# Weight preparation without GpSimd, scale copies in DRAM, and single modulations in a two-layer feed-forward kernel

## The reference

```python
# x (64, 64, 512), cond (64, 256); b2, b3, b_up, b_down are biases
q_emb = relu(cond @ W3 + b3)                                   # one gate per batch and feature
z     = (64 * x + sum_n(x)) * q_emb[:, None, :]
x1    = relu(z @ W2 + b2)
w_up   = ((w_up_q - 7.5)   * repeat(w_up_scale, 64, axis=1)).T      # 512 x 2048
w_down = ((w_down_q - 7.5) * repeat(w_down_scale, 64, axis=1)).T    # 2048 x 512
x2  = relu(x1 @ w_up + b_up + x1 @ up_a @ up_b)
out = x + x2 @ w_down + b_down + x2 @ down_a @ down_b
```

## Time and profile before

| | |
|---|---|
| median of three runs | 848.18 us (842.65 to 849.38) |
| the profiled execution's own time | 847.49 us |
| its span, first to last instruction | 845.7 us, mean granted TensorE clock 0.968 |
| busy: TensorE, VectorE, ScalarE, GpSimd | 767.0, 553.7, 422.1, 95.5 us |

### The profile page before, as it was taken

The page is one execution under the profiler, slowest core; times in us unless marked ns, Lnnn a source line. Parts: engine busy times, 40 slices in busy tenths (PEclk is TensorE's granted clock), DMA queues, the critical chain, the costliest instruction groups (busy, mean ns, idle before and its releaser), DMA issues.

```text
span 845.7 us, 9583 instructions
## 1 busy us (share of the span) xinstructions
PE 767.0 (91%) x3248; PEld 620.2 (73%) x3248; DVE 553.7 (65%) x705; ACT 422.1 (50%) x734; POOL 95.5 (11%) x81
## 2 busy tenths in 40 slices
PE   6379887878889999999999999998999999999997
PEld 5268665766668787777778887787878886888875
DVE  5665547646556567766677679575866769666575
ACT  3856234535534526375665726565755544343441
POOL 2441132232221202000000002000000002000000
PEclk9789999999899999999999999999999999999999
DMA  9714675775765659666551678565650786665552
GB/s 304 275 47 138 210 232 155 232 215 173 212 175 164 211 187 396 202 208 224 175 174 50 235 242 319 200 203 197 208 188 27 258 304 239 210 184 177 199 172 100
DMA packets 92144, 169.55 MB, mean 200 GB/s; under 512 B 8768, under 2 KB 25280, under 8 KB 91456
## 3 DMA queue, kind: packets, MB, share of 16 engines
q1 hardware_dynamic: 91808, 168.86, 60.8%
q10 hardware_dynamic: 288, 0.08, 0.0%
HBM read 129.05 MB, written 39.85 MB: 200 GB/s over the span
## 4 chain that ended last, share of the span: by engine, by line
PE 58%; DVE 14%; DMA 12%; ACT 8%; issue 5%; SPq 3%; DVEq 0%; ACTq 0%
PE ps L1073 19%; PE ps L1074 19%; PE ps L1075 19%; DMA scale<-in_scales 12%; ACT xt L364 4%; DVE x_lo L891 3%; DVE made L758 2%; DVE whole L749 2%; SPq L264 1%; DVE x_sum L795 1%; DVE x2p_lo L766 1%; ACT xm_hi L376 1%; SPq L258 1%; DVE xt L720 1%; DVE res L781 1%
## 5 line engine op out<-in xcount | busy, mean ns | idle before, releaser
L1073 PE MATMUL ps<-x_hi,ring 128*128 128x512 f32 x672 | 266.4, 396 | 18.6 <-ACT ps L481 10.2
L1074 PE MATMUL ps<-x_lo,ring 128*128 128x512 f32 x672 | 264.2, 393 | 0.0
L1075 PE MATMUL ps<-x_hi,ring 128*128 128x512 f32 x672 | 264.0, 393 | 0.0
L1073 PEld LDWEIGHTS ps<-x_hi,ring 128*128 128x128 f32 x672 | 127.6, 190 | 54.2 <-ACT ps L481 14.2
L1075 PEld LDWEIGHTS ps<-x_hi,ring 128*128 128x128 f32 x672 | 127.7, 190 | 26.9
L1074 PEld LDWEIGHTS ps<-x_lo,ring 128*128 128x128 f32 x672 | 127.7, 190 | 25.9
L364 ACT ACTIVATE xt<-xt,gated,gate_n 128x64 f32<-128x64 f32 x224 | 76.7, 428 | 104.5 <-DVE gated L714 104.5
L891 DVE TENSOR_TENSOR x_lo<-x_sum,x_hi 128x512 fp32r<-128x512 f32 (+1 forms) x96 | 82.8, 883 | 12.6 <-ACT x_hi L497 8.6
L473 ACT ACTIVATE f<-ps,bias 128x512 f32<-128x512 f32 x96 | 64.7, 690 | 41.2 <-PE ps L1075 41.2
L851 DVE TENSOR_TENSOR res<-ps,res 128x512 f32<-128x512 f32 x72 | 48.5, 688 | 30.7 <-PE ps L1075 30.7
L822 DVE TENSOR_TENSOR ps<-s,ps 128x512 f32<-128x512 f32 x48 | 33.3, 693 | 52.4 <-PE ps L1075 48.0
(11 more groups left out here) (79 smaller groups left out, 1049.9 us busy)
## 6 DMA issues: line engine op xcount, KB each, us to landing
ring<-made_w SPq DMA_DIRECT2D x336, 256.0 KB, 3.8
made_w<-made SPq DMA_DIRECT2D x16, 1280.0 KB, 5.9
xt<-in_x SPq DMA_DIRECT2D x32, 256.0 KB, 5.4
code<-in_codes SPq DMA_DIRECT2D x16, 512.0 KB, 7.6
scale<-in_scales SPq DMA_DIRECT2D x32, 256.0 KB, 8.2
res<-in_x SPq DMA_DIRECT2D x4, 2048.0 KB, 9.8
made_w<-plain SPq DMA_DIRECT2D x64, 128.0 KB, 6.1
out<-res SPq DMA_DIRECT2D x12, 512.0 KB, 5.7
```

The costliest lines, as they stand in the source:

```text
L1073: pe.matmul(dest, w_hi, a_hi, start=start, stop=False, skip_group_check=True)
L1074: pe.matmul(dest, w_hi, a_lo, start=False, stop=False, skip_group_check=True)
L1075: return pe.matmul(dest, w_lo, a_hi, start=False, stop=stop, skip_group_check=True)
```

## The change

1. Scales: one DMA early in the prologue copies each scale row eight times into a DRAM tensor `made_s`; each unit's scales are then one DMA that reads 16 rows, each eight times. A third scale buffer lies in the space of `s4`.
2. SyncE's loop of stage 1: `load_scale(u+4)` and `load_codes(u+3)` stand ahead of the two stores of unit u; `load_res(0)` moves into the loop.
3. GpSimd has no instruction left. Its sums (`made_totals`), the low parts of W2 and of the tables, and the residual fix (`fix_c22`, four operations of 512 columns a block, two by each of the first D slots) are VectorE's. The tables lie in three quadrants instead of four with a smaller part to split, and the wide one is cast and split in two pieces.
4. The prologue's order is written out anew: gates in four PSUM banks with a signal each; of the second half, eighth 5 is modulated on VectorE; `low_rank(0)` stands behind the first step of the second half, `low_rank(1)` behind the last, and `low_rank(u+2)` behind the second tile of unit u instead of ahead of unit u.
5. Stage 1's loops on VectorE and ScalarE are reordered (below); block 1's input is modulated in units 4 to 11.
6. Blocks 1 and 2: one modulation in each of the slots 3, 4, 6, 7, 8, 10, 11, 12; sum and gate stand right behind `share`; the input loads begin at slot 0 instead of 3.
7. Last block: ("U", 7) stands ahead of ("D", 2, 0); the operands of units 6 and 7 get buffers of their own in the space of x1, free after the last product of ("U", 7), and their steps are reordered.

```diff
-            ("U", 5), ("U", 6), ("D", 2, 0), ("U", 7), ("D", 2, 1), ("D", 3, 0), ("D", 3, 1)]
+            ("U", 5), ("U", 6), ("U", 7), ("D", 2, 0), ("D", 2, 1), ("D", 3, 0), ("D", 3, 1)]
...
+    MODULATED = [3, 4, 6, 7, 8, 10, 11, 12]
+
+
+    def x2_set(s, p):
+        return p % 2 + (2 if s == SBS - 1 and p >= NP - 2 else 0)
...
+        x2_place = [("x2", 0), ("x2", 28672), ("x1", 0), ("x1", 28672)]
+        x2_hi = [sb(f"x2_hi{v}", [P, 7, T], F32R, over, skip) for v, (over, skip) in enumerate(x2_place)]
...
+        made_s = nc.dram_tensor("made_s", [UNITS, 2, COPIES, 1024], F32, kind="Internal").ap()
...
             def load_scale(u):
-                if u >= 2:
-                    sp.wait_ge(dequantized, u - 2 + 1)
-                for h in range(2):
-                    sp.dma_start(scale[u % 2][64 * h:64 * h + 64, :],
-                                 scales[uid(FIRST[u]), h:h + 1, :].to_broadcast([64, 1024])).then_inc(scale_loaded[u % 2], 16)
+                if u >= 3:
+                    sp.wait_ge(dequantized, u - 3 + 1)
+                rows = made_s[uid(FIRST[u])].rearrange("h c v -> (h c) v").unsqueeze(1)
+                sp.dma_start(scale[u % 3][:], rows.to_broadcast([2 * COPIES, P // 2 // COPIES, 1024])).then_inc(scale_loaded[u % 3], 16)
...
+                if k == 1:
+                    sp.dma_start(made_s, scales.unsqueeze(2).to_broadcast([UNITS, 2, COPIES, 1024])).then_inc(scales_copied, 16)
...
+            load_x(0, KD)
+            load_x(0, KD + 1)
             load_codes(0)
+            sp.wait_ge(scales_copied, 16)
             load_scale(0)
-            for k in range(KD):
-                load_x(0, KD + k)
-            load_codes(1)
-            load_scale(1)
-            load_codes(2)
+            load_x(0, KD + 2)
+            load_x(0, KD + 3)
+            for u in (1, 2):
+                load_codes(u)
+                load_scale(u)
             sp.wait_ge(w2_split, KD)
             for k in range(KD):
                 sp.dma_start(made_w2[k], w2_in_ring[k][:].rearrange("p h v -> p (h v)").bitcast(F32)).then_inc(w2_stored, 16)
-            sp.wait_ge(tab_split, 3)
-            load_res(0)
+            load_scale(3)
             for u in range(UNITS):
-                if u + 2 < UNITS:
-                    load_scale(u + 2)
+                if u + 4 < UNITS:
+                    load_scale(u + 4)
+                if u + 3 < UNITS:
+                    load_codes(u + 3)
+                if u == 0:
+                    sp.wait_ge(tab_split, 3)
+                    load_res(0)
                 store_plain(u)
                 if 2 <= u < 10:
                     load_x(1, u - 2)
                 store_made(u)
-                if u + 3 < UNITS:
-                    load_codes(u + 3)
...
-                    if s < SBS - 1 and 3 <= n < 11:
-                        load_x(s + 1, n - 3)
+                    if s < SBS - 1 and n < 8:
+                        load_x(s + 1, n)
...
-                if p >= 2:
+                if x2_set(s, p) >= 2:
+                    act.wait_ge(prod[M6], chain_no(s, ("U", NP - 1)) + 1)
+                elif p >= 2:
...
                     if unit[0] == "U":
                         full_tile(u, 0)
+                        full_tile(u, 1)
+                    if 4 <= u < 12:
+                        x_modulate(1, u - 4)
+                    if u >= 12:
+                        x_high(1, 2 * (u - 12))
+                        x_high(1, 2 * (u - 12) + 1)
                     made_high(u)
-                    if unit[0] == "U":
-                        full_tile(u, 1)
-                    if 3 <= u < 11:
-                        x_modulate(1, u - 3)
-                    if 11 <= u < 13:
-                        x_high(1, 2 * (u - 11))
-                        x_high(1, 2 * (u - 11) + 1)
                     if unit[0] == "U":
                         full_tile(u, 2)
...
+            def made_totals(u):
+                w = whole[u % 3][:].rearrange("p (i q a c) -> p i q a c", i=2, q=2, a=2)
+                to = made_sum[:, u % 2, :, 1, :].rearrange("p v (q c) -> p v q c", q=2)
+                dve.wait_ge(whole_done, 2 * u + 2)
+                if u >= 2:
+                    dve.wait_ge(made_stored[u % 2], 16 * (u // 2))
+                dve.tensor_tensor(to[:, 0:2].rearrange("p a q c -> p q a c"), w[:, 0], w[:, 1], ALU.add).then_inc(made_summed, 1)
+                dve.tensor_tensor(to[:, 2], w[:, 0, :, 0, :], w[:, 1, :, 1, :], ALU.add).then_inc(made_summed, 1)
+                dve.tensor_tensor(to[:, 3], w[:, 0, :, 1, :], w[:, 0, :, 0, :], ALU.subtract).then_inc(made_summed, 1)
+                dve.tensor_tensor(to[:, 4], w[:, 1, :, 0, :], w[:, 1, :, 1, :], ALU.subtract).then_inc(made_summed, 1)
...
+            def fix_c22(s, dd):
+
+                to = res[:, dd + 2, 1, :]
+                dve.wait_ge(res_loaded, 16 * s + 16)
+                dve.tensor_tensor(to, to, res[:, dd, 1, :], ALU.subtract).then_inc(res_fixed, 1)
+                dve.wait_ge(res_fixed, 4 * (s - 1) + 2 * dd + 1)
+                dve.tensor_tensor(to, to, res[:, dd + 2, 0, :], ALU.add).then_inc(res_fixed, 1)
...
+            x_low(0, 3)
+            lora_low()
+            wide_low(slice(0, T), 2)
+            x_sum(0, 5)
+            x_shift(5)
+            x_modulate(5)
+            x_sum(0, 6)
+            x_gate(0, 6)
+            x_sum(0, 7)
+            x_gate(0, 7)
+            dequantize(0)
+            x_low(0, 4)
+            add_lora(0)
+            x_low(0, 5)
+            x1p_low(0, 0)
+            x1p_low(0, 2)
+            x_low(0, 6)
+            dequantize(1)
+            x_low(0, 7)
+            plain_low(0)
...
+            wide_low(slice(T, NH * P), 3)
+            add_lora(1)
             x1p_low(1, 0)
             x1p_low(1, 2)
-            add_lora(1)
+            made_totals(0)
...
                 if u < 14:
                     plain_low(u + 1)
-                    if u + 2 < UNITS:
-                        dequantize(u + 2)
                 evacuate(u, 0)
-                if u + 2 < UNITS:
-                    add_lora(u + 2)
                 evacuate(u, 1)
+                if 4 <= u < 12:
+                    x_sum(1, u - 4)
+                    x_gate(1, u - 4)
+                if u < 14:
+                    dequantize(u + 2)
+                if 12 <= u < 14:
+                    x_low(1, 2 * (u - 12))
+                    x_low(1, 2 * (u - 12) + 1)
                 if u < 14:
                     made_low(u)
+                    add_lora(u + 2)
                 if u == 14:
                     x1_lows_late(1)
-                if 3 <= u < 11:
-                    x_sum(1, u - 3)
-                    x_gate(1, u - 3)
                 evacuate(u, 2)
-                if 11 <= u < 13:
-                    x_low(1, 2 * (u - 11))
-                    x_low(1, 2 * (u - 11) + 1)
                 evacuate(u, 3)
+                if u < 14:
+                    made_totals(u + 1)
...
+                    if not last and n in MODULATED:
+                        x_sum(s + 1, MODULATED.index(n))
+                        x_gate(s + 1, MODULATED.index(n))
+                    if unit[0] == "D" and unit[1] == 0:
+                        fix_c22(s, unit[2])
...
+                    if t == 1 and u + 2 < UNITS:
+                        low_rank(u + 2)
```

More of the change, by code:

```diff
@@ L656, in _ @@
                         x2_high(s, (n - 1) // 2, 4)
+                    if n == 12 and last:
+                        x2_high(s, 6, 2)
+                    if n == 13 and last:
+                        x2_high(s, 7, 2)
                     if not last and n in (8, 10):
@@ L892, in x2_low @@
+                dve.tensor_tensor(x2_lo[z][:, low:high, :], source, x2_hi[z][:, low:high, :].bitcast(F32),
                                   ALU.subtract).then_inc(x2_split[v], 1)
-            for k in range(KD):
-                x_sum(0, k)
-                if k > 0:
-                    x_low(0, k - 1)
-                x_modulate(k)
-            x_low(0, KD - 1)
+            x_sum(0, 0)
+            x_shift(0)
+            x_modulate(0)
+            w2_low(0)
+            x_sum(0, 1)
+            x_shift(1)
@@ new lines, in _ @@
+            x_low(0, 0)
+            x_modulate(1)
+            w2_low(1)
+            x_sum(0, 2)
+            x_shift(2)
+            x_low(0, 1)
+            x_modulate(2)
+            w2_low(2)
+            x_sum(0, 3)
+            x_shift(3)
+            x_low(0, 2)
+            x_modulate(3)
+            w2_low(3)
+            x_sum(0, 4)
+            x_gate(0, 4)
+            x_low(0, 3)
[3 more added lines that the diff above has]
+            x_shift(5)
@@ L903, in _ @@
                                      op1=ALU.subtract).then_inc(bias_done, 1)
-            for k in range(KD):
-                x_sum(0, KD + k)
-                x_gate(0, KD + k)
-                if k > 0:
-                    x_low(0, KD + k - 1)
-            dequantize(0)
-            x_low(0, 2 * KD - 1)
```

(18 more changed lines are left out.)

249 lines of the change are left out of this document (121 added, 128 removed).

## The result

| | before | after |
|---|---|---|
| median of four runs each, same chip | 848.46 us (842.65 to 849.38) | 770.89 us (768.87 to 771.69) |
| ratio, 95% interval | | 0.9095 (0.9051 to 0.914) |
| profiled execution's own time, span, clock | 847.49, 845.7, 0.968 | 768.87, 766.8, 0.996 |
| first matmul of unit 0 | 59.33 | 47.75 (-11.6) |
| units 0 to 13, to the first of ("W", 1) | 206.5 | 166.3 (-40.2) |

What follows compares the result with a forecast made beforehand. TensorE bounds blocks 1 to 3; the loop of `made_low`, store, scale load and `dequantize` bounds units 0 to 13. From 847.5 us, -13 - 39 + 1 - 23 = -74 gives 773.5; range 757 to 796.

Steps and rivals of the forecast that it cites:

- Term 1: Prologue: unit 0 starts at 46.5 instead of 59.3, -13 us; bounds of that start 44 to 53.
- Term 2: Block 0's units 0 to 13: scale-load loop gone, stage 167.6 us including a 3.6 stall, instead of 206.5: -39.
- Case 4: Rival for units 0 to 13: VectorE inherits the wait for stored sums; slower than before, 913 us; chance 0.03.
- ("W", 1) and units 14 and 15: End of block 0, 44.7 us with TensorE full: VectorE gets one more `made_totals`, +1 us.
- Term 3: Blocks 1 to 3: gaps and low clock removed, -23 us.
- (a): Blocks 1 to 3: residual fix off GpSimd stops stretching VectorE's operations; gain 6 us of gaps, 4 of clock.
- (b): Blocks 1 and 2: single modulations, gate behind `share`, remove six waits for `pass_c11`; 9.5 us, plus 2 of clock.
- (c): Last block: the 2.03 us gap and its clock, 2, give way to about 2 us of small stalls; gain 2.
- (d): Blocks 1 to 3: input loads starting at slot 0 cost nothing; if cover fails, +6 us.
- Case 2: Rival: stalls of blocks 1 and 2 move instead of going; Term 3 gives 10 instead of 23, 786.5 us; chance 0.12.
- Case 5: Rival: copies leave scale loads as slow, only lengthening the queue; counted with VectorE or DMA setting block 0's pace, 0.15.
- sign of a partial inflation: VectorE beside GpSimd: `made_low` averages 1.50 against 1.42 us, so GpSimd's stretching of VectorE's operations is only partial.

Runs made afterwards that it cites:

- b1: Kernel before, with only codes and scales of unit u+3 issued ahead of the stores of unit u on SyncE: 814.03 us, 0.9609.
- a2: Changed kernel with SyncE's old order of scale and code loads, behind the store of the unit before: 778.73 us, 0.9197.
- a1: Changed kernel without the copies of the scales in DRAM; each scale load reads the input again: 765.37 us, 0.9042.
- c1: Changed kernel with block 1's input modulated behind the last tile of its unit and no copies in DRAM: 757.79 us, 0.8933.
- a7: Changed kernel with the modulation of block 1's input moved on ScalarE behind the last tile of its unit: 762.89 us, 0.9013.
- a5: Changed kernel with the residual fix back on GpSimd, two operations of 1024 columns a block: 782.53 us, 0.9219.
- b2: Kernel before, modulations still in pairs, with only sum and gate of the next block's input moved right behind `share`: 833.77 us, 0.9823.
- a4: Changed kernel with modulations of blocks 1 and 2 in pairs again in slots 4, 8 and 12, sum and gate still behind `share`: 770.91 us, 0.9084.
- a8: Changed kernel with order, buffers and steps of the last block as before: 770.79 us, 0.9086.
- a3: Changed kernel with only the sums of quarters (`made_totals`) back on GpSimd: 764.80 us, 0.9015.
- c2: c1 with `x_modulate(0, 6)` later on ScalarE and `x_low(0, 4)` earlier on VectorE in the prologue: 753.80 us, 0.8891.

## Why the prediction was right, step by step

**Bound.** Both readings of the trace of before held. Blocks 1 to 3 were TensorE's with 31 us of gaps and low clock: 26.9 of them are gone. Units 0 to 13 were held by the store ahead of the scale load: b1, which changes only that order, takes 32.2 us off the stage, and a2, which changes it back, brings VectorE's waits for scales back (40.9 us in 12 places).

**Term 1, prologue: -13 forecast, -11.6 measured.** The first half was done (last matmul at 25.33, forecast near 26.5) and the second began (30.47, forecast near 31) as rebuilt. From there two errors cancel in part. That the second half "is held by ScalarE" did not show: the one further pause, 1.81 us at 37.36, is VectorE's, whose `add_lora(0)` waited for `low_rank(0)`, and from 37.36 to unit 0 TensorE does not wait. And the sum of 46.5 left the copy out, yet without it unit 0 starts at 44.89 (a1) and 41.62 (c1), so the rest of the term was too large and the copy made up for it. The clock cost a little more than the 2 us put in. From 31.17 to 34.16 and from 37.70 to 40.68 seven matmuls each start 0.43 us apart, which is 14 x 0.2 = 2.8 us over the upper level. The copy, put at 4 us beside the sum, at most 8, costs about 3 in the profile (a1), and 5 in the times of a7 and c1. Of the prologue's other edits none was tried alone; which of them give the 11.6 us is not shown.

**Term 2, units 0 to 13: -39 forecast, -40.2 measured, but by two wrong terms that cancel.**
- "A unit needs 0.94 us for its low-rank matmuls" is wrong. The unstalled unit takes 11.38 us, of which 48 x 0.227 = 10.9 are its own, so low-rank matmuls cost 0.5. The 0.94 of the earlier trace rows was read at a place where the four matmuls themselves waited for `add_lora` in their middle: 1.10 us for the four there, 0.64 for four that do not wait. TensorE alone needs 159.3 us (a7), not 164.
- The stall is 7.0 us (166.3 - 159.3), not 3.6. The loop itself was right, 12.7 forecast and 12.62 measured, but against 11.38 instead of 11.85 VectorE falls behind by 1.24 us a unit instead of 0.85.
- `made_totals`, taken as 1.65 within 1.5 to 4.1, measures 1.6 (161.67 - 160.06, from the first sum to `plain_low`). GpSimd's prices for quarters say nothing of VectorE's.
- The wait for stored sums didn't show: idle time 0.0 ahead of L780. Case 4 fell at its first condition. At 160.06 the sums needed the buffer whose store SyncE had issued at 145.16; such a store takes 5.9 us to land (median), so there were some 9 us to spare.

**("W", 1) and units 14 and 15: +1 forecast, 0 measured.** The one `made_totals` more is covered.

**Term 3, blocks 1 to 3: -23 forecast, -26.9 measured.** This is where most of the missing 4.6 us of own time (773.5 - 768.87) lies. (a) The fix: 6 + 4 = 10 forecast, 9.9 by a5, where the clock fell behind one of the three gaps. Before it fell behind two (0.59 from 526 to 530, 0.57 from 711 to 715), and one such stretch costs 1.6 to 1.7 us (matmuls 0.43 us apart instead of 0.227 over some 3.5 us). (b) The gaps of `pass_c11`: 9.5 + 2 = 11.5 forecast, 13 by b2. The clock is not what was missed: it fell behind one of the six, as forecast (403 to 407). But a gap costs more than its idle time: at 403.06 the matmul before had started at 400.40 and the next starts at 403.39, so the two steps take 2.54 us more than undisturbed ones (2.99 - 2 x 0.227) where the idle time is 2.27. Six times the difference of 0.27 is 1.6 us. The cause was put as "one modulation each, and its gate behind `share`"; a4 and b2 show it was the gate alone. The predicted 2.75 us from halving the pair were not needed. (c) 2 forecast, 2.4 by a8's profile. The three make 25.3, and the second stretch of low clock that a5 did not bring back is the other 1.6. (d) Early loads cost nothing that shows. Case 2, that the stalls move, is out: no TensorE gap in blocks 1 and 2 is over 0.2 us.

**Case 5** was right as a mechanism though not as a danger. The copies leave the scale loads as slow (median 7.7 us to landing, against 7.3 in a1, the same order without copies, and 8.2 before), and a1 shows that the loads don't need to be faster once they are asked for early.

**GpSimd and VectorE.** In the earlier trace rows and a5 an operation with two SBUF inputs is stretched while GpSimd works: `x_low` of 512 columns from 0.69 to 2.73 us. This agrees with the Trainium skill, "SBUF — State Buffer", reading the diagram, which names operations with two SBUF inputs as those that take the shared pair, and says the loser blocks. The prediction's sign of a partial inflation, `made_low` at 1.50 against 1.42 us, was a misreading: 1.42 is the piece of it that stands on the chain, 1.50 the mean duration of the whole operation, and the one on the chain lasts 1.49 too (129.84 in order of time). With GpSimd empty `made_low` lasts 1489 ns, with it in the kernel before 1504, so it was hardly stretched there. Yet the rule isn't a price. a3 pays it in full (1792 ns for `made_low`) and is 6 us faster: the loop loses 1.6 us of sums and gains some 0.3 in `made_low`, which leaves it under TensorE's 11.38; a5 pays it where TensorE waits next, and loses 10.

## What to carry to other kernels

Find the loop that closes across engines, and count only what stands on it: moving a cheap operation (1.6 us of sums, a 2.8 us modulation) off the loop's in-order lists was worth 6 to 7 us here, while scale loads made faster and a GpSimd emptied of its sums were worth nothing. In a DMA queue's list, put loads that wait for little ahead of stores that wait for much; that reordering alone gave 32 us. Read the price of an operation where it does not wait: a group of four instructions can hide a stall between its members.

## What was not expected of the hardware

- One list of instructions has more than one prologue. In five profiled kernels whose lists are the same up to unit 0, it starts at 47.75 (the changed kernel), 49.51 (a4), 48.75 (a5), 48.98 (a7) and 48.90 (a8); between a1 and c1 it is 44.89 and 41.62. In the latter pair the clock fell to 0.58 in one and stayed at 1.00 in the other, behind pauses of like length. What decides it was not found out. Such a pause of TensorE cost some 3 us more or nothing; in c2, where it is 0.63 us, the clock did not fall. The times of c1 show it too: of its five runs the fastest (756.02 us, the profiled one) has a mean clock of 0.999, the slowest (759.61) 0.995. The profiled execution of the changed kernel is likewise its fastest.
- GpSimd stretched VectorE's operations only where both inputs lie in SBUF. In b1 `plain_low` takes 1.74 us beside GpSimd's sums (139.60; alone 1.22), while `add_plain`, which reads PSUM, takes its usual 0.68 us in the middle of one:

```profile
141.89 1.72 POOL L691 TENSOR_TENSOR made_sum<-whole 128x256 f32<-128x256 f32 x1
142.94 0.68 DVE L781 TENSOR_TENSOR res<-ps,res 128x512 f32<-128x512 f32 x1
```

- A unit's scales as two DMAs of 256 KB, each 64 partitions reading one DRAM row, took a median of 8.2 us each to land before and 7.3 in a1; as one DMA of 512 KB, sixteen rows read eight times each, 7.7.
